# A gated delta rule in chunks on one Trainium2 core: three stages over couples instead of two, with rows of v and k made by TensorE

## The chip, the cores and the metric

The kernel runs on one core of one Trainium2 chip. The time is the device time of one whole execution in microseconds (us). The kernel before takes 4307.55 us, the median of 3 runs (4305.54 to 4310.32). TensorE is PE in the profile, its weight loads are PEld; VectorE is DVE, ScalarE is ACT, GpSimd is POOL, and SP issues the transfers.

## The reference, cut to what matters

Two layers run over 4096 tokens of width 256. The change touches one part, the gated delta rule of the first layer: 16 heads, keys and values of 64, one state of 64 x 64 for each head.

```
def step(S, inp):
    q_t, k_t, v_t, g_t, b_t = inp
    Sk = einsum('bhkv,bhk->bhv', S, k_t)
    delta = einsum('bhv,bhk->bhkv', v_t, k_t) - einsum('bhv,bhk->bhkv', Sk, k_t)
    S = exp(g_t)[..., None, None] * S + b_t[..., None, None] * delta
    o_t = einsum('bhkv,bhk->bhv', S, q_t)
    return (S, o_t)
_, o = scan(step, S0, (q, k, v, g, beta))      # then o @ Wo.T
```

The rest (norm and router, projections with a short convolution, experts, second norm, the last attention) is the same in both kernels.

## The kernel before, in words

The program is a row of phases, one after the other; `phase_delta` is the third. It works on chunks of C = 64 tokens, two chunks (x = 0 and 1) are a couple, and there are 32 couples. A tile `[P, NPAIR, C]` holds all 16 heads: two heads share the 128 partitions (64 each), 8 pairs lie along the free dimension. One "group" of TensorE work is `over_heads` over one `product`: 16 products of 64 x 64 by 64 x 64 in f32, all recorded at line 863, and the trace shows each product as two weight loads and two matmuls, so a group is 32 + 32 instructions. `over_heads` can take two products and then interleaves them one by one, which makes a pair of groups.

What is computed for a chunk: (1) `keys_keys`, the products of keys with keys, masked and scaled into `upper` (`take_upper`, `minus_eye`); (2) the inverse of that triangular matrix by five doublings, level k = 1 to 5, each `half` (PE), `mask_step` (DVE), `up` (PE), `turn_low` (DVE) and `keep_inverse` (ACT); (3) `keys_queries`, masked into `qk` (`attention`, DVE); (4) the state's part, a chain from chunk to chunk: `residual` (k_g times the state) into the bank `pd_r`, subtracted on DVE from the rows of v (L1180), `updates` (PE), `take_updates` (u, DVE L1193), `decay_updates` (u_dec = u times the decay, POOL L1301), `new_state` (k_row times u_dec, PE) and `take_state` (DVE L1198), beside it `old_outputs` and `new_outputs` into `pd_o`, and `project` (L939, 64 instructions of which half are matmuls of 256 columns) once a couple in two parts.

The rows of k and v come from elsewhere: k and v are loaded with the channel on the partitions, a transpose on DVE turns them in blocks of 32 (L1170, L1175), and ACT copies the blocks to their places in 8 small copies for each chunk and each of the two (L1100 `keep_rows`, L1109 `keep_values`).

The order is written out by hand and unrolled over 33 iterations. Iteration `it` has `post` = couple it (state part), `pre` = couple it+1 (inverse) and `ahead` = couple it+2 (its loads, decays, `grow`, `rel`). On PE `keys_keys(ahead)` is paired with the last `up` of `pre`, and masking and the first inverse follow at the top of the next iteration, in front of the first `half`. Every engine runs its own list in order and waits on semaphores; there is no loop instruction in the phase. SP issues all loads of a couple: 8 transfers of 128 KB (sums, sums_k), k, v and q of 512 KB each, and 128 KB of rows. The core of the list on PE at the top of an iteration:

```
new, asked = over_heads(updates(post, 0), keys_queries(pre, 1))
wait_half(pre, 0, 1);  wait_outputs(post, 0)            # the second waits for u
low, out = over_heads(half(pre, 0), new_outputs(post, 0))
wait_half(pre, 1, 1);  wait_new(post, 0)                # the second waits for u_dec
low, new = over_heads(half(pre, 1), new_state(post, 0))
```

Of the kernel before, what the change touches and what calls it, by code (L numbers as in the profile page):

```python
# [14 lines left out]
P = 128  # L15
T = 4096
D = 256
# [32 lines left out]
def shape_constants():  # L50
# [14 lines left out]
    for n in range(LEVELS):  # L65
# [6 lines left out]
        "couples": -couples - eye_c, "doublings": np.concatenate(doublings[1:], 1), "eye_c": eye_c,  # L72
        "iota": np.tile(np.arange(NE), (P, 1)).astype(float),
# [608 lines left out]
def phase_delta(nc, g, ctx):  # L682
# [19 lines left out]
    KEY_LOADS = 9  # L702
# [8 lines left out]
    upper = [sb(f"upper{x}", W) for x in range(2)]  # L711
    k_g = sb("k_g", [P, 4, NPAIR, C])
    qk = sb("qk", [P, 4, NPAIR, C])
    inv = [sb(f"inv{x}", W) for x in range(2)]
    inv_low = [sb(f"inv_low{x}", W) for x in range(2)]
    k_turned = [sb(f"k_turned{x}", W) for x in range(2)]
    v_turned = [sb(f"v_turned{x}", W) for x in range(2)]
    v_row = sb("v_row", [P, 2, NPAIR, C])
    step = [sb(f"step{x}", W) for x in range(2)]
    inv_fin = sb("inv_fin", [P, 4, NPAIR, C])  # L720
# [3 lines left out]
    u_dec = sb("u_dec", W)  # L724
# [10 lines left out]
    k_in, q_in, v_in = ([sem(f"{n}_in{r}") for r in range(2)] for n in "kqv")  # L735
# [4 lines left out]
    kt_d, vt_d, values_d, minus_d = (sem2(s) for s in ("kt", "vt", "values", "minus"))  # L740
    res_d, ress_d, w_d, u_d, udec_d, o_d, ocp_d = (sem(s) for s in ("res", "ress", "w", "u", "udec", "o", "ocp"))
# [3 lines left out]
    kk_d, qk_d, upper_d, att_d, inv1_d, rows_d = (sem2(s) for s in ("kk", "qk", "upper", "att", "inv1", "rows"))  # L745
# [3 lines left out]
    def heads():  # L749
        for p in range(NPAIR):  # L750
            for h in range(2):
                yield p, slice(h * C, (h + 1) * C)
# [7 lines left out]
    B32 = C // 2  # L760
    SAME, OTHER = range(2)

    def blocks_of(h):

        to = (1 - h) * C
        for a in range(2):
            for b in range(2):
                yield (slice(h * C + b * B32, h * C + (b + 1) * B32), slice(a * B32, (a + 1) * B32),
                       slice(to + a * B32, to + (a + 1) * B32), slice(b * B32, (b + 1) * B32))

    class Couple:


        def __init__(self, eng, c, odd, uses):
            keep = (lambda value: value) if isinstance(c, int) else eng.to_reg
            self.c, self.first = c, isinstance(c, int) and c < 2
            self.now, self.last = keep(c + 1), keep(c)
            self.level = [keep(c * NL + n) for n in range(NL + 1)]
            self.chunk = [c * 2 + x for x in range(2)]
            self.begun = [keep(c * 2 + x) for x in range(2)]  # L780
            self.ended = [keep(c * 2 + x + 1) for x in range(2)]
            self.stated = [keep(c * 2 + x + 2) for x in range(2)]
            self.older = None if self.first else [keep(c * 2 + x - 3) for x in range(2)]
            self.before = None if self.first else keep(c - 1)
            self.previous = [keep(c * 2 + x - 1) for x in range(2)] if c > 0 else None
            self.key_loads = keep(uses * (16 * KEY_LOADS))
            self.odd, self.filled = odd, keep(uses * 16)
            self.emptied = None if self.first else keep(uses * 32 - 32)
            self.ring = [odd * 2 + x for x in range(2)]

    def fixed(eng, c):
        return Couple(eng, c, c % 2, c // 2 + 1) if 0 <= c <= LAST else None

    def couples(engine, one):


        for it in range(-1, LAST + 1):
            one(fixed(engine, it), fixed(engine, it + 1), fixed(engine, it + 2))
# [3 lines left out]
    @block.sync  # L802
    def _(sp):
        sp.dma_start(wo[:], g.given["wo_t"].rearrange("(n p) d -> p n d", p=P)).then_inc(wo_in, 16)
# [5 lines left out]
        def load_keys(n):  # L810
            for x in range(2):
                for h in range(2):
                    for dst, half in ((sums, h), (sums_k, 1 - h)):
                        sp.dma_start(dst[half * C:(half + 1) * C, x].rearrange("p n t -> p (n t)"),
                                     spread(g.sums_d[bass.ds(n.chunk[x], 1), h, :], [C, NPAIR * C])).then_inc(k_in[n.odd], 16)
            load("k", k_t, n).then_inc(k_in[n.odd], 16)

        def load_rows(n):
            if not n.first:
                sp.wait_ge(scattered[n.odd], n.emptied)  # L820
            sp.dma_start(rows[:, n.odd, :], g.xn_d[bass.ds(n.c * P, P), :]).then_inc(rows_in[n.odd], 16)

        load_keys(fixed(sp, 0))
        load("q", q_t, fixed(sp, 0)).then_inc(q_in[0], 16)
        load("v", v_t, fixed(sp, 0)).then_inc(v_in[0], 16)
        load_rows(fixed(sp, 0))

        def one(post, pre, ahead):
            if ahead is None:
                return  # L830
            if post is not None:
                for x in range(2):
                    sp.wait_ge(qk_d[x], post.now)
                    sp.wait_ge(kt_d[x], post.now)
                    sp.wait_ge(kg_d[x], post.now)
                    sp.wait_ge(grow_d[x], post.now)
            if pre is not None:
                for x in range(2):
                    sp.wait_ge(diff_d[x], pre.now)
                    sp.wait_ge(grow_d[x], pre.now)  # L840
            load_keys(ahead)
            if post is not None:
                for x in range(2):
                    sp.wait_ge(vt_d[x], post.now)
            load("v", v_t, ahead).then_inc(v_in[ahead.odd], 16)
            if post is not None:
                sp.wait_ge(o_d, post.ended[1])
            load("q", q_t, ahead).then_inc(q_in[ahead.odd], 16)
            load_rows(ahead)

        couples(sp, one)
        for r in range(2):
            sp.wait_ge(scattered[r], (LAST + 1) // 2 * 32)

    @block.tensor
    def _(pe):
# [16 lines left out]

        def wait_keys(n, x):
            wait_each(pe, (k_in[n.odd], n.key_loads))

        def keys_keys(n, x, p, h):
            r = n.ring[x]
            return product(p, h, p_pre[x], OTHER, of_couple(k_t, r), of_couple(k_t, r))

        def wait_queries(n, x):
            wait_each(pe, (q_in[n.odd], n.filled), (up_d[x], n.level[0]))

        def keys_queries(n, x, p, h):
            r = n.ring[x]
            return product(p, h, p_low[x], OTHER, of_couple(k_t, r), of_couple(q_t, r))

        def wait_half(n, x, k):
            if k == 1:
                wait_each(pe, (minus_d[x], n.now))  # L890
            wait_each(pe, (lowc_d[x], n.level[k]))

        def half(n, x, p, h):
            return product(p, h, p_pre[x], SAME, of(upper[x]), of(inv_low[x]))

        def wait_up(n, x, k):
            if k == 1:
                wait_each(pe, (inv1_d[x], n.now), (att_d[x], n.now))
            else:
                wait_each(pe, (up_d[x], n.level[k - 1]))  # L900
            wait_each(pe, (step_d[x], n.level[k]))

        def up(n, x, p, h):
            return product(p, h, p_low[x], SAME, of(step[x]), of(inv[x]))

        def wait_state(n, x):
            wait_each(pe, (kg_d[x], n.now), (qg_d[x], n.now), (ocp_d, n.begun[x]), (state_d, n.ended[x]))

        def residual(n, x, p, h):
            return product(p, h, p_r, OTHER, of(k_g, n.ring[x]), of(state))  # L910

        def old_outputs(n, x, p, h):
            return product(p, h, p_o, SAME, of(state), of_couple(q_t, n.ring[x]), start=p == 0, stop=False, shared=True)

        def wait_updates(n, x):
            wait_each(pe, (tok_d, n.last), (up_d[x], n.level[NL]), (ress_d, n.ended[x]))

        def updates(n, x, p, h):
            return product(p, h, p_u, SAME, of(inv_fin, n.ring[x]), of(resid))

        def wait_outputs(n, x):
            wait_each(pe, (att_d[x], n.now), (u_d, n.ended[x]))

        def new_outputs(n, x, p, h):
            return product(p, h, p_o, OTHER, of(u), of(qk, n.ring[x]), start=False, stop=p == NPAIR - 1, shared=True)

        def wait_new(n, x):
            wait_each(pe, (rows_d[x], n.now), (udec_d, n.ended[x]))

        def new_state(n, x, p, h):  # L930
            return product(p, h, p_n, OTHER, of(k_row, x), of(u_dec))

        def project(n, pairs):
            out = p_u[:].rearrange("p n t -> p (n t)")
            if pairs[0] == 0:
                wait_each(pe, (wo_in, 16), (ocp_d, n.ended[1]))
# [7 lines left out]

# [1627 lines left out]
```

## Time and profile before

| what | value |
| --- | --- |
| median of 3 runs | 4307.55 us |
| the profiled execution's own time | 4308.53 us |
| its span (first to last instruction) | 4306.8 us |
| PE busy / PEld busy | 3878.8 us (90%) / 2318.4 us (54%) |
| DVE / ACT / POOL busy | 3062.9 / 2444.4 / 1101.5 us |
| instruction queue q8 | 424 packets, 6.95 MB |
| the delta phase | about 560 to 1800 us of the span |

The page gives busy time by engine, then the span in 40 slices (each digit a tenth), then the transfer queues. A busy PE is not a PE at its peak, since matmuls overlap. Queue q8 carries instructions, not data. The word "issue" in a row says that an engine stood idle while no semaphore that the profile knows held it.

### The profile page before, as it was taken

Reading aid. Unit: us, or ns where it says so; the run is one execution under the profiler, and the core shown is the slowest. Engines: PE = TensorE matmul, PEld = TensorE weight load, DVE = VectorE, ACT = ScalarE, POOL = GpSimd, SP = SyncE. Lnnn points to the kernel's source line nnn. Section 1 sums busy time; section 2 is a strip of 40 time slices with the busy share of each in tenths; the row PEclk is TensorE's granted clock in tenths of the full one; section 3 lists DMA queues with packets and bytes.
Section 4 is the critical chain, followed back from the end, with each engine's and each line's share of the span. In section 5 each row is a group of like instructions: output and inputs, shape, how many; then the busy total and the mean of one; then the engine's idle time right before and its main releaser. Section 6 shows DMA issues by size and latency. Waiting matters only on the chain. (4 is left out here: it accounts for less than half of the span.)

```text
span 4306.8 us, 128467 instructions
## 1 busy us (share of the span) xinstructions
PE 3878.8 (90%) x52237; PEld 2318.4 (54%) x52237; DVE 3062.9 (71%) x5127; ACT 2444.4 (57%) x3901; POOL 1101.5 (26%) x1106
## 2 busy tenths in 40 slices
PE   5999778888888788897887999999999999999998
PEld 4444377777777777676664344444444444444443
DVE  5799855555555555444896787878878787878786
ACT  2788655656655565434442465656656565656554
POOL 1000055655555555201777000000000000000000
PEclk9999889989899998999897899999999999999999
DMA  3544532222222222225345000000000000000000
GB/s 126 184 125 120 150 101 86 88 74 83 83 85 85 72 87 81 61 85 154 100 111 132 8 5 19 4 9 15 10 14 10 13 5 19 5 17 6 10 15 10
DMA packets 271802, 265.28 MB, mean 62 GB/s; under 512 B 53761, under 2 KB 232065, under 8 KB 270497
## 3 DMA queue, kind: packets, MB, share of 16 engines
q1 hardware_dynamic: 250768, 226.07, 17.6%
q0 software_dynamic: 6144, 16.79, 1.2%
q10 hardware_dynamic: 14352, 14.55, 1.0%
q8 instruction: 424, 6.95, 0.7%
q14 instruction: 114, 0.93, 0.1%
HBM read 151.95 MB, written 105.38 MB: 60 GB/s over the span
## 5 line engine op out<-in xcount | busy, mean ns | idle before, releaser
L2358 DVE TENSOR_REDUCE part_max<-p_m 128x1 f32<-128x512 f32 x2118 | 1362.9, 685 | 378.5 <-PE p_m L2200 371.0
L2340 ACT ACTIVATE prob<-p_s 128x1024 f32<-128x1024 f32 x1024 | 1047.7, 1023 | 748.2 <-PE p_s L2264 746.1
L2219 PE MATMUL p_o<-prob,v_one 128*64 128x512 f32 x4096 | 1054.6, 592 | 3.9 <-ACT prob L2340 0.5
L2200 PE MATMUL p_m<-keys,queries 96*64 96x512 f16 x4236 | 661.7, 387 | 28.0 <-DMA keys<-parts_d 20.4
L2264 PE MATMUL p_s<-queries,keys 97*64 97x512 f16 x4096 | 619.4, 380 | 0.0
L2264 PEld LDWEIGHTS p_s<-queries,keys 97*64 97x64 f16 x4096 | 228.8, 109 | 597.6 <-issue 592.8
L863 PE MATMUL pd_pre<-inv_low,upper 64*64 64x64 f32 x10240 | 397.3, 234 | 103.1 <-issue 56.5
L2168 POOL TENSOR_TENSOR attn<-o_num,o_inv 32x512 f32<-32x512 f32 x64 | 81.0, 1265 | 1458.6 <-DVE o_inv L2377 1452.1
L863 PEld LDWEIGHTS pd_pre<-inv_low,upper 64*64 64x64 f32 x10240 | 364.3, 147 | 120.7 <-issue 115.5
L2200 PEld LDWEIGHTS p_m<-keys,queries 96*64 96x64 f16 x4236 | 239.1, 108 | 309.9 <-DVE part_max L2358 56.3
L863 PE MATMUL pd_low<-inv,step 64*64 64x64 f32 x10240 | 373.2, 229 | 26.8 <-issue 24.9
L863 PEld LDWEIGHTS pd_low<-inv,step 64*64 64x64 f32 x10240 | 349.0, 144 | 59.6 <-issue 57.7
L2219 PEld LDWEIGHTS p_o<-prob,v_one 128*64 128x64 f32 x4096 | 288.4, 136 | 162.5 <-issue 15.8
L588 PE MATMUL p_proj<-xn_t_all,proj_w_sb 128*128 128x512 f32 x768 | 337.8, 596 | 7.7 <-PEq L2503 7.7
L1118 ACT ACTIVATE inv<-pd_low 128x512 f32<-128x512 f32 x256 | 152.7, 597 | 333.4 <-DVE inv_low L1212 332.4
L1204 DVE TENSOR_TENSOR step<-pd_pre,const 128x512 f32<-128x512 f32 x320 | 215.5, 679 | 85.9 <-PE pd_pre L863 82.0
L1212 DVE STREAM_TRANSPOSE inv_low<-pd_low 128x512 f32<-128x512 f32 x256 | 181.4, 709 | 127.9 <-PE pd_low L863 127.8
L588 PEld LDWEIGHTS p_proj<-xn_t_all,proj_w_sb 128*128 128x128 f32 x768 | 146.9, 191 | 192.9 <-issue 187.7
L1100 ACT ACTIVATE k_row<-k_turned 32x256 f32<-32x256 f32 x512 | 211.9, 414 | 6.9
L1109 ACT ACTIVATE v_row<-v_turned 32x256 f32<-32x256 f32 x512 | 211.8, 414 | 6.9
L1301 POOL TENSOR_TENSOR u_dec<-u,rel 128x512 f32<-128x512 f32 x64 | 67.7, 1058 | 290.8 <-DVE u L1193 290.8
L2377 DVE RECIPROCAL o_inv<-o_raw 128x64 f32<-128x64 f32 x256 | 137.8, 541 | 0.0
(235 smaller groups left out, 5725.2 us busy)
## 6 DMA issues: line engine op xcount, KB each, us to landing
q_d<-conv_q SPq DMA_DIRECT2D x16, 1024.0 KB, 5.0
v_d<-conv_v SPq DMA_DIRECT2D x16, 1024.0 KB, 5.0
k_d<-conv_k SPq DMA_DIRECT2D x16, 1024.0 KB, 6.5
sums<-sums_d SPq DMA_DIRECT2D x128, 128.0 KB, 3.1
sums_k<-sums_d SPq DMA_DIRECT2D x128, 128.0 KB, 3.4
k_t<-k_d SPq DMA_DIRECT2D x32, 512.0 KB, 4.9
q_t<-q_d SPq DMA_DIRECT2D x32, 512.0 KB, 3.6
v_t<-v_d SPq DMA_DIRECT2D x32, 512.0 KB, 5.3
```

Source lines behind the costliest of these rows:

```text
L588: last = te.matmul(p_proj[u % RING][:], g.proj_w_sb[:, n, c, p * P:(p + 1) * P], g.xn_t[:, c, b * BLK:(b + 1) * BLK], start=c == 0, stop=c ...
L863: return te.matmul(out[rows_of(h if to == SAME else 1 - h), p, :], lhs(p, rows_of(h)), rhs(p, rows_of(h)), start=start, stop=stop, skip_gr ...
L1100: last = a.activation(k_row[to_p, x, :, to_t], k_turned[x][from_p, :, from_t], ACT.Copy)
L1109: last = a.activation(v_row[to_p, x, :, to_t], v_turned[x][from_p, :, from_t], ACT.Copy)
L1118: a.activation(inv[x][:] if k < NL else inv_fin[:, n.ring[x]], p_low[x][:], ACT.Copy).then_inc(up_d[x], 1)
L1204: v.tensor_tensor(step[x][:], p_pre[x][:], over_pairs(masks[:, k - 1, :]), ALU.mult).then_inc(step_d[x], 1)
L1212: v.transpose(inv_low[x][:], p_low[x][:]).then_inc(lowc_d[x], 1)
L2200: last = te.matmul(p_m[k % 2][x * HALF:(x + 1) * HALF, :], queries[0:ROW, p, hh, at:at + HALF], keys[0:ROW, 2 * p + hh, kb * BLK:(kb + 1) ...
L2219: product = te.matmul(p_o[64 * hh:64 * hh + VW, :], g.v_one[:, j, p, hh:hh + 2, :].rearrange("p a d -> p (a d)"), prob[:, j % 2, hh, :], s ...
L2264: last = te.matmul(p_s[j % 2][x * HALF:(x + 1) * HALF, hh, :], keys[0:KR, 2 * p + hh, at:at + HALF], queries[0:KR, p, hh, :], start=True, ...
L2340: a.activation(prob[:, j % 2], p_s[j % 2][:], ACT.Exp, scale=SCORE_SCALE).then_inc(exp_d, 1)
L2358: v.tensor_reduce(part_max[:, hh * SUB + sub, kb:kb + 1], p_m[k % 2][:], AX.X, ALU.max).then_inc(red_d, 1)
```

## The change

`phase_delta` is written anew around the same arithmetic. The loop runs over 34 iterations from -2.

1. Stages: `keys_keys(ahead)` moves to the middle of the iteration, into the banks `pd_r` and `pd_n`, and `take_upper`, `minus_eye`, `first_inverse` and `turn_first` of `ahead` are done within the same iteration, two couples ahead of the state part; `upper` becomes a ring of four. The last-but-one inverse goes to a new tile `inv_half`.
2. Rows by TensorE: `key_rows` and `values` are products of k and v with the identity (`eye_c`, and a new constant `less_eye`, the negative). The 4 DVE transposes and 32 small ACT copies of a couple go; `take_rows` (DVE) multiplies the rows of k by the decay while it takes them from the bank, so that `decay_updates` on POOL goes and `new_state` waits for u alone.
3. `values` leaves minus v in `pd_r`, `residual` adds to it there, and ACT takes it with scale -1 (`residual` on ACT); the DVE subtraction goes.
4. The order on PE: nearly every group of the state part is paired with one of the inverse, 14 pairs and 10 groups alone. The order before has 9 pairs and 16 groups alone.
5. Loads: sums, k, sums_k, v, rows, q, each behind its own wait. The bytes are the same.

```
+    def values(n, x):
+        return lambda p, h: product(p, h, p_r, OTHER, of_couple(v_t, n.ring[x]), of_const("less_eye"), start=p == 0, stop=False, shared=True)
+    def key_rows(n, x):
+        return lambda p, h: product(p, h, p_o if x == 0 else p_n, OTHER, of_couple(k_t, n.ring[x]), of_const("eye_c"))
+    def residual(n, x):                                   # PE
+        return lambda p, h: product(p, h, p_r, OTHER, of(k_g, x), of(state), start=False, stop=p == NPAIR - 1, shared=True)
-    v.tensor_tensor(resid[:], v_row[:, x], p_r[:], ALU.subtract).then_inc(ress_d, 1)
+    a.activation(resid[:], p_r[:], ACT.Copy, scale=-1.0).then_inc(ress_d, 1)
+    v.tensor_tensor(k_row[:, x], (p_o if x == 0 else p_n)[:], spread(rel[:, n.ring[x], :, C:C + 1], W), ALU.mult)
-    po.tensor_tensor(u_dec[:], u[:], spread(rel[:, n.ring[x], :, C:C + 1], W), ALU.mult).then_inc(udec_d, 1)
```

The new list on PE, a line for each group or pair (the semaphore waits ahead of each are left out):

```
half(pre,0)+residual(post,0)      half(pre,1)+keys_queries(pre,0)
old_outputs(post,0)               updates(post,0)+values(post,1)
up(pre,0,1)                       up(pre,1,1)+new_outputs(post,0)
half(pre,0)+new_state(post,0)     half(pre,1)
up(pre,0,2)+residual(post,1)      up(pre,1,2)+keys_queries(pre,1)
old_outputs(post,1)               updates(post,1)
half(pre,0)                       half(pre,1)+new_outputs(post,1)
up(pre,0,3)+new_state(post,1)     up(pre,1,3)+keys_keys(ahead,0)
half(pre,0)+keys_keys(ahead,1)    half(pre,1)+key_rows(pre,0)
project, first part               up(pre,0,4)+key_rows(pre,1)
up(pre,1,4)+values(pre,0)         half(pre,0)   half(pre,1)
project, second part              up(pre,0,5)   up(pre,1,5)
```

## Rows read from the trace of the kernel before

**Rows 1.** The page: busy time, then the slices of PE and its granted clock.
```profile
PE 3878.8 (90%) x52237; PEld 2318.4 (54%) x52237; DVE 3062.9 (71%) x5127; ACT 2444.4 (57%) x3901; POOL 1101.5 (26%) x1106
PE   5999778888888788897887999999999999999998
PEclk9999889989899998999897899999999999999999
```

**Rows 2.** Stretches: length, busy us (instructions) of each engine, clock, transfer share, GB/s.
```profile
560.00:1780.00 1220.00, 1014.29 (x35249) 923.99 (x35248) 704.58 (x1075) 716.80 (x1534) 694.02 (x653) 0.92 0.25 78
1365.60:1380.90 15.30, 13.89 (x509) 13.34 (x508) 10.83 (x17) 9.02 (x20) 6.24 (x7) 0.89 0.18 53
1433.90:1439.87 5.97, 2.87 (x126) 2.63 (x127) 1.99 (x3) 5.18 (x13) 1.63 (x2) 1.00 0.61 196
1419.30:1424.90 5.60, 5.44 (x125) 4.67 (x126) 2.23 (x4) 2.37 (x5) 4.59 (x5) 1.00 0.12 31
1467.14:1469.20 2.06, 2.06 (x71) 1.99 (x66) 1.88 (x3) 1.19 (x2) 0.81 (x1) 1.00 0.03 8
1471.03:1473.10 2.07, 2.07 (x141) 2.07 (x143) 0.69 (x1) 0.98 (x2) 0.46 (x2) 1.00 0.65 216
```

**Rows 3.** One line's instructions, once a couple: duration ns, first and last start.
```profile
L1134 ACT ACTIVATE attn_tok<-pd_u x32: 383/383/387, 619.7 to 1805.6; 128x256 f32<-128x256 f32 x32
```

**Rows 4.** Transfer queues, stretch 560 to 1780: packets, MB, share of 16 engines.
```profile
q1 hardware_dynamic: 36514, 82.65, 21.2%
q8 instruction: 279, 4.57, 1.6%
```

**Rows 5.** Order of time, PE: start, us, group, count, idle before it and releaser.
```profile
1421.87 1.95 PE L939 MATMUL pd_u<-wo,o_t 128*64 128x256 f32 x16
...
1439.87 0.21 PE L863 MATMUL pd_u<-resid,inv_fin 64*64 64x64 f32 x1 [3.07 <-issue]
...
1459.25 0.62 PE L863 MATMUL pd_pre<-inv_low,upper 64*64 64x64 f32 x13
1461.64 1.73 PE L863 MATMUL pd_pre<-inv_low,upper 64*64 64x64 f32 x51 [1.78 <-issue]
...
1489.19 0.32 PE L863 MATMUL pd_pre<-inv_low,upper 64*64 64x64 f32 x4
1490.91 0.51 PE L863 MATMUL pd_pre<-inv_low,upper 64*64 64x64 f32 x10 [1.40 <-issue]
```

**Rows 6.** Transfer queues, stretch 1365.6 to 1380.9.
```profile
q8 instruction: 4, 0.07, 2.2%
```

**Rows 7.** Transfer queues, stretch 1432.5 to 1437.5, whole answer's queue part.
```profile
DMA packets 499, 1.38 MB, mean 277 GB/s; under 512 B 72, under 2 KB 72, under 8 KB 499
q1 hardware_dynamic: 499, 1.38, 88.2%
```

**Rows 8.** Waits, 560 to 1780: us in total, times, longest.
```profile
PE pd_pre L863 <- issue: 59.1, 55, 2.6
PE pd_low L863 <- issue: 49.8, 63, 3.8
PE pd_pre L863 <- DVE u L1193: 29.4, 30, 1.2
PE pd_o L863 <- issue: 20.1, 17, 2.7
```

**Rows 9.** Groups of instructions, 560 to 1780: busy us, mean ns, idle before.
```profile
L1109 ACT ACTIVATE v_row<-v_turned 32x256 f32<-32x256 f32 x504 | 208.5, 414 | 6.8
L1180 DVE TENSOR_TENSOR resid<-v_row,pd_r 128x512 f32<-128x512 f32 x62 | 42.6, 687 | 54.1 <-PE pd_r L863 54.1
L1123 ACT ACTIVATE o_t<-pd_o 128x512 f32<-128x512 f32 x62 | 36.9, 595 | 52.4 <-PE pd_o L863 52.2
L1301 POOL TENSOR_TENSOR u_dec<-u,rel 128x512 f32<-128x512 f32 x62 | 65.6, 1058 | 270.4 <-DVE u L1193 270.4
L1297 POOL TENSOR_TENSOR inv<-upper,const 128x512 f32<-128x512 f32 x62 | 78.6, 1267 | 4.4
```

More of the change, by code:

```diff
@@ L791, in fixed, with __init__ @@
[L791 to L798, printed above, removed]
+    class Couple:
+        def __init__(self, c):
+            self.c, self.odd = c, c % 2
+            self.now, self.last, self.before = c + 1, c, c - 1
+            self.level = [c * NL + n for n in range(NL + 1)]
+            self.chunk = [c * 2 + x for x in range(2)]
+            self.begun = [c * 2 + x for x in range(2)]
+            self.ended = [c * 2 + x + 1 for x in range(2)]
+            self.previous = [c * 2 + x - 1 for x in range(2)]
+            self.older = [c * 2 + x - 3 for x in range(2)]
+            self.filled = (c // 2 + 1) * 16
+            self.emptied = c // 2 * 32
+            self.ring = [self.odd * 2 + x for x in range(2)]
@@ L800, in phase_delta, with couple, couples @@
+    def couple(c):
+        return Couple(c) if 0 <= c <= LAST else None
+    def couples(one):
+        for it in range(-2, LAST + 1):
+            one(couple(it), couple(it + 1), couple(it + 2))
     block = ctx.enter_context(nc.Block())
@@ L808, in load @@
             return sp.dma_start(dst[:, n.odd].rearrange("p n x t -> p n (x t)"), src)
[L810 to L826, printed above, removed]
         def one(post, pre, ahead):
@@ L903, in up @@
[L903 to L913, printed above, removed]
@@ L960, in first_part, with one @@
-        def first_part(post, pre):
+                    for i, one_product in enumerate(products):
+                        if one_product is not None:
+                            last[i] = one_product(p, h)
+            return last
+        def one(post, pre, ahead):
+            if pre is not None:
+                wait_half(pre, 0, 1)
             if post is not None:
-                wait_state(post, 0)
-                _, last = over_heads(lambda p, h: old_outputs(post, 0, p, h), lambda p, h: residual(post, 0, p, h))
-                last.then_inc(res_d, 1)
+                wait_residual(post, 0)
+            low, res = over_heads(half(pre, 0) if pre is not None else None, residual(post, 0) if post is not None else None)
@@ new lines, in one @@
+            if post is not None:
+                wait_old(post, 0)
+                over_heads(old_outputs(post, 0))
+                wait_updates(post, 0)
+                wait_values(post, 1, None)
+                new, kept = over_heads(updates(post, 0), values(post, 1))
+                new.then_inc(w_d, 1)
+                kept.then_inc(val_d, 1)
+            if pre is not None:
+                wait_up(pre, 0, 1)
+                over_heads(up(pre, 0, 1))[0].then_inc(upmm_d[0], 1)
+                wait_up(pre, 1, 1)
@@ L1069, in _ @@
-        for x in range(2):
-            wait_keys(fixed(pe, 0), x)
-            over_heads(lambda p, h: keys_keys(fixed(pe, 0), x, p, h))[0].then_inc(kk_d[x], 1)
+                wait_old(post, 1)
+                over_heads(old_outputs(post, 1))
+                wait_updates(post, 1)
+                over_heads(updates(post, 1))[0].then_inc(w_d, 1)
+            if pre is not None:
+                wait_half(pre, 0, 3)
+                over_heads(half(pre, 0))[0].then_inc(half_d[0], 1)
+                wait_half(pre, 1, 3)
@@ new lines, in one @@
+            if post is not None:
+                wait_outputs(post, 1)
+            low, out = over_heads(half(pre, 1) if pre is not None else None, new_outputs(post, 1) if post is not None else None)
+            if pre is not None:
+                low.then_inc(half_d[1], 1)
+            if post is not None:
+                out.then_inc(o_d, 1)
+            if pre is not None:
+                wait_up(pre, 0, 3)
+            if post is not None:
+                wait_new(post, 1, pre)
+            raised, new = over_heads(up(pre, 0, 3) if pre is not None else None, new_state(post, 1) if post is not None else None)
@@ new lines, in one @@
+            if pre is not None:
+                raised.then_inc(upmm_d[0], 1)
+            if post is not None:
+                new.then_inc(new_d, 1)
+            if pre is not None:
+                wait_up(pre, 1, 3)
+            if ahead is not None:
+                wait_keys(ahead, 0)
+            raised, keyed = over_heads(up(pre, 1, 3) if pre is not None else None, keys_keys(ahead, 0) if ahead is not None else None)
+            if pre is not None:
+                raised.then_inc(upmm_d[1], 1)
@@ new lines, in one @@
+            if pre is not None:
+                wait_half(pre, 1, 4)
+                wait_key_rows(pre, 0, ahead)
+                low, turned = over_heads(half(pre, 1), key_rows(pre, 0))
+                low.then_inc(half_d[1], 1)
+                turned.then_inc(kr_d[0], 1)
+            if post is not None:
+                project(post, range(0, NPAIR // 2))
+            if pre is not None:
+                wait_up(pre, 0, 4)
+                wait_key_rows(pre, 1, ahead)
+                raised, turned = over_heads(up(pre, 0, 4), key_rows(pre, 1))
+                raised.then_inc(upmm_d[0], 1)
+                turned.then_inc(kr_d[1], 1)
+                wait_up(pre, 1, 4)
+                wait_values(pre, 0, ahead)
+                raised, kept = over_heads(up(pre, 1, 4), values(pre, 0))
+                raised.then_inc(upmm_d[1], 1)
+                kept.then_inc(val_d, 1)
+                for x in range(2):
+                    wait_half(pre, x, 5)
+                    over_heads(half(pre, x))[0].then_inc(half_d[x], 1)
@@ L1072, in _ @@
+            if post is not None:
+                project(post, range(NPAIR // 2, NPAIR))
+            if pre is not None:
+                for x in range(2):
+                    wait_up(pre, x, 5)
+                    over_heads(up(pre, x, 5))[0].then_inc(upmm_d[x], 1)
         pe.wait_ge(g.const_in, 16)
-        couples(pe, one)
+        couples(one)
     @block.scalar
@@ L1126, in one @@
             if post is not None:
-                keep_rows(post, 0)
-                keep_values(post, 1)
-                keep_outputs(post, 0)
-                keep_rows(post, 1)
-            for k in range(1, NL + 1):
-                if k == NL and post is not None:
-                    act.wait_ge(proj_d, post.now)
-                    a.activation(g.attn_tok[:, bass.ds(post.c, 1), :].rearrange("p a d -> p (a d)"),
-                                 p_u[:].rearrange("p n t -> p (n t)")[:, 0:D], ACT.Copy).then_inc(tok_d, 1)
-                if pre is not None:
+                residual(post, 0)
@@ new lines, in one @@
+            if pre is not None:
+                for x in range(2):
+                    grown(pre, x)
+            if ahead is not None:
+                related(ahead, 0)
+            if pre is not None:
+                for x in range(2):
+                    keep_inverse(pre, x, 1)
+            if post is not None:
+                keep_outputs(post, 0)
+            if ahead is not None:
+                related(ahead, 1)
+            if post is not None:
+                residual(post, 1)
@@ L1137, in one @@
+            if pre is not None:
+                for x in range(2):
+                    keep_inverse(pre, x, 2)
+            if post is not None:
+                keep_outputs(post, 1)
+            if pre is not None:
+                for k in (3, 4):
                     for x in range(2):
                         keep_inverse(pre, x, k)
[L1139 to L1143 removed]
@@ L1144, in one @@
-                if k == 3:
-                    if post is not None:
-                        keep_outputs(post, 1)
-                    if ahead is not None:
-                        for x in range(2):
-                            related(ahead, x)
-        for x in range(2):
-            grown(fixed(act, 0), x)
-            related(fixed(act, 0), x)
-        couples(act, one)
+            if post is not None:
+                act.wait_ge(proj_d, post.now)
+                a.activation(g.attn_tok[:, bass.ds(post.c, 1), :].rearrange("p a d -> p (a d)"),
+                             p_u[:].rearrange("p n t -> p (n t)")[:, 0:D], ACT.Copy).then_inc(tok_d, 1)
@@ L1156, in _ @@
+            if pre is not None:
+                for x in range(2):
+                    keep_last_inverse(pre, x)
+        couples(one)
     @block.vector
```

556 lines of the change are left out of this document (267 added, 289 removed).

## The prediction

> **What bounds the kernel now.** I read the page first, for where the time is: PE is busy nearly everywhere, and from about slice 6 to slice 17, where the clock digit drops to 8 and 9, runs the only phase that the change touches [rows 1]. The stretch view gives its size: 1220 us between 560 and 1780, PE busy 1014 of them, DVE 705, ACT 717, POOL 694 [rows 2]. Three engines are idle for 40% of it, so PE's list sets the time, and the question is what holds PE.
>
> The period first. `attn_tok` is written once a couple, 32 times between 619.7 and 1805.6 [rows 3]; that is 38.3 us a couple, and as the last iteration is a short one (the state part alone), about 38.7 for a full iteration. In it PE executes 34 groups of 64 instructions and 64 of `project`, 2240. What would they take if nothing but the array counted? Two groups alone, one behind the other, took 2.06 us, and two pairs 2.07 us for twice the instructions, the last two rows of their group [rows 2]. So a group alone and a pair both cost 1.03 us: the second member of a pair is free for the array. `project` took 1.95 us a part [rows 5]. Before: 16 alone + 9 pairs = 25 x 1.03 + 2 x 1.95 = 29.7 us. The 9.0 us to 38.7 are what has to be explained.
>
> The waits name little of it: 29.4 us in all are for u, 0.95 us a couple; most of the rest is "issue", 59.1 + 49.8 + 20.1 us and smaller ones [rows 8]. The order of time shows what those are. At 1459.9 PE stops after 13 matmuls of a row of `half` and goes on with the next at 1461.64; no semaphore stands inside a group. At 1489.5 the same for 1.40 us, and in the middle of an `updates` for 3.07 us [rows 5]. The transfer queues give the cause: q8, which carries instructions, moved 279 packets in the 1220 us, 4.57 MB, so 16 KB each [rows 4]. PE executed 35249 + 35248 instructions there [rows 2], 253 to a packet, with the semaphore waits beside them about 256 of 64 bytes. One block of instructions lands every 4.37 us on average. Four blocks were fetched and 1017 instructions executed in a calm stretch of 15.3 us, 3.83 us each, and in that stretch both paired and single groups ran [rows 2, 6]. One block took 5.97 us with PE busy for 2.87 of them; for 5 us of that, k, v and sums kept the transfer engines 88% busy and q8 moved nothing [rows 7]. One took 5.60 us because it held a part of `project`, whose few instructions are long [rows 2].
>
> So I read it thus: **PE is fed at about 3.83 us for a block of 256 instructions**, whether these are paired (the array would need 1.8 us) or not (3.7 us), and more when a burst of loads or long instructions fall in. By that, before is 2240 / 253 = 8.86 blocks x 3.83 = 33.9 us, and 4.8 us of excess: bursts, `project`, the waits for u and u_dec.
>
> The Trainium skill says otherwise of the price: the page Runtime: NRT & Kernel Launch, section Instruction fetch mechanics, has blocks of 16 KiB, 256 instructions, fetched ahead while the current one runs, at a cost "mostly hidden". The trace agrees with the size of the block and not with the hiding: 1.40 and 1.78 us of standstill in the middle of a group [rows 5]. What the rule would make of this change is the fourth rival.
>
> **The change part by part.**
>
> *Groups on PE.* `values` and `key_rows` add 2 + 2 groups a couple: 256 instructions, all in pairs. For the array they are free: 14 pairs + 10 alone = 24 x 1.03 + 3.9 = 28.6 us, 1.1 less than before. For the feeding they are a full block: 2496 / 253 = 9.87 blocks. Price of a block between 1.84 us (pairs at the array's rate, 2.07 x 253 / 284) and 5.97 (in a burst); I take the calm stretch's 3.83, since it has the mix of both kinds: 9.87 x 3.83 = 37.8, **+3.9 us a couple**.
>
> *What goes from PE's path.* `new_state` waits no more for u_dec (POOL, 1.06 us, behind other POOL work [rows 9]), and between `updates` and `new_outputs` a group `up` is put (1.03 us), which covers the 0.69 us of u: the 0.95 us a couple of waits for u go, **-0.95**. The u_dec wait lies mostly inside the fetch of the same block, as the top of the iteration is also where the loads burst [rows 7]; I count 0 for it, and -1.1 at the most.
>
> *`project`.* Its first part now has pairs on both sides, 1.95 us + 221 instructions at pair rate (1.6) = 3.6, below 3.83, so its block costs no more than any other; the second still has `half` and `up` alone round it. The block with a part cost 5.60 against 3.83 but the next one then comes early, so of the 1.8 I take half: **-0.9**. Ends: 0 and -1.8.
>
> *The other engines.* ACT loses 32 small copies of 414 ns a couple, 13.2 us, and gets 2 of about 0.6 for the residual; DVE loses 4 transposes and 2 subtractions of about 0.68 and gets 2 `take_rows`; POOL loses 2 x 1.06 [rows 9]. All three idle 40% now, PE waits for them rarely, so 0. The covers stay: ACT's residual is 0.60 instead of DVE's 0.69 and has `old_outputs` (1.03) beside it.
>
> *Moved steps and added waits.* `pd_n` now serves in turn `keys_queries`, `new_state`, `keys_queries`, `new_state`, `keys_keys`, `key_rows`, each waiting for DVE to empty it: 6 x (1.15 + 0.69) = 11 us of turns in a period near 40. The tightest is `keys_keys(ahead, 1)`, which waits for `take_state(1)` one pair after `new_state(1)`; `half` of level 4 is queued behind it. By the array's rate it would stand up to about 1 us; fed at 3.83 a block (a pair each 1.9) the wait is over when its instructions come. I take 0, upper end +1. POOL's list is about 21 us an iteration (18 operations of 1.05 to 1.28, [rows 9], and the scatter), DVE's 24 x 0.69: neither is near 40. `first_inverse` (1.27 us on POOL, [rows 9]) and `turn_first` leave the top, where the first `half` follows them; as that is where the burst holds the block anyway, 0, with -1.3 as the end.
>
> *Loads.* Same 2.9 MB a couple, asked for in another order: sums, k and sums_k still together at the top. The bursts, 2 to 2.5 blocks a couple, stay: 0, from -1 (spread out) to +1 (k, v and sums meet more fetches). Start and end: one more short iteration, but the same chain to the first `half`: 0, +/- 5 us once. 64 more constant columns: 32 KB, nothing.
>
> *Sum.* 3.9 - 0.95 - 0.9 = +2.05 us a couple, 40.8 in place of 38.7; x 31 full iterations = +64 us. On the profiled execution's 4308.5 us (span 4306.8) that is 4372; this execution is 1.0 us above the median of the runs, which changes nothing I can claim. **Forecast 4372 us.**
>
> **The rivals.**
> 1. *The excess grows with the blocks.* Each block costs the average 4.37 us, not 3.83 plus a fixed rest: 9.87 x 4.37 = 43.1, +4.4 x 31 = +137: **4445**. For: a burst hits whichever fetch is under way, and with shorter work a block more of them end in a standstill. Against: the waits for u are plainly not tied to blocks.
> 2. *Faster: the chain's waits were the excess.* The mechanism is the top of the iteration, `updates`, u, u_dec, `new_state` in single file: if they, and not the loads, made the 5.97 us blocks, the whole 4.8 goes as the new order covers them all: 37.8, -0.9 x 31 = **4280**. It decides from the point where more than 3.9 of the 4.8 us go. For: u_dec waited 270 us for u, PE for both. Against: q8 moved nothing for 5 us while data did [rows 7], and the long block ran to its end on the fetch.
> 3. *A draw.* 3.9 gained and lost: **4308**.
> 4. *Blocks are hidden*, and PE's standstills have another cause which thinner lists of ACT and DVE remove: 28.6 us of array work and some 2 of waits, -8 x 31: **4060**. Against: standstills inside a group.
>
> **How the numbers follow.** Forecast 0.50; rival 1 0.17; rival 2 0.22; draw 0.07; rival 4 0.04. This kernel's measurement can tell 0.2%, 8.6 us, from no change. Slower: 0.50 + 0.17, faster: 0.22 + 0.04 and 0.01 of the draw, same 0.06. The range takes the forecast's open terms (-1.1 - 0.9 - 1 to +0.9 + 1 + 1 a couple, not all at once) and reaches into both neighbours: 4275 to 4455.
>
> **What would show it.** PE's instructions in the phase up by 8192, q8's packets in it by about 32, to some 310. The period of `attn_tok` from 38.3 to 40 or 41. "Issue" idle of PE up by 30 us or more with standstills inside pairs, the row of PE waiting for u gone, ACT's and DVE's busy time down by 380 and 80 us without effect. Wrong would be: blocks coming faster than 3.5 us on average, or a period under 38.

## The result, and the profile after

The changed kernel takes 4340.39 us (median of 4 runs, 4335.22 to 4350.06), the kernel before beside it 4308.93 us: ratio 1.0076, 95% interval 1.0055 to 1.0097. It is 31 us slower, where 64 were forecast. On the chip of a later batch the kernel before took 4358 us and the changed one 4346 us, a ratio of 0.9979 (0.9968 to 0.9991): there the change is a small gain. The changed kernel is nearly the same on both (4340, 4346); it is the kernel before that moved by 49 us. So each experiment below is read against the kernel before of its own batch, and as a difference: the times in the expectations reckon from 4309 or 4340 us. The granted clock goes with it: over a whole run it is 0.952 to 0.957 in the kernel before where it takes 4305 and 0.944 to 0.949 where it takes 4358, and 0.964 to 0.971 in the changed kernel on either.

The page after, the same three lines as [rows 1]:

```profile
PE 3834.0 (88%) x56333; PEld 2258.0 (52%) x56333; DVE 2981.2 (69%) x4999; ACT 2057.0 (47%) x2941; POOL 1035.6 (24%) x1042
PE   5999777777777777799687999999999999999998
PEclk9999899999999999999898899999999999999999
```

PE has 4096 more matmuls and 4096 more weight loads, and is busy 45 us less; ACT is busy 387 us less, DVE 82 us less, and none of that came back as time. The stretch of the phase, columns as in [rows 2]:

```profile
560.00:1820.00 1260.00, 965.71 (x38977) 859.25 (x38978) 617.43 (x940) 333.09 (x590) 627.28 (x589) 0.96 0.24 76
```

The line written once a couple, against 619.7 to 1805.6 in [rows 3]:

```profile
L1204 ACT ACTIVATE attn_tok<-pd_u x32: 384/384/386, 619.5 to 1845.9; 128x256 f32<-128x256 f32 x32
```

That is (1845.9 - 619.5) / 31 = 39.56 us a couple, 1.31 more than 38.25. The start is the same to 0.2 us, and from the last of these lines to the end of the span it is 2502.4 us against 2501.2: the whole difference of the two profiled executions (4350.06 and 4308.53 us) lies in the iterations of the delta phase.

The waits of PE, same view as [rows 8], over 560 to 1800:

```profile
PE pd_pre L836 <- issue: 79.4, 56, 3.4
PE pd_low L836 <- issue: 69.1, 57, 2.1
PE pd_n L836 <- issue: 45.8, 40, 2.4
PE pd_o L836 <- issue: 25.7, 23, 2.6
PE pd_r L836 <- issue: 25.2, 24, 2.1
PE pd_low L836 <- DVE step L1255: 10.9, 17, 1.2
PE pd_pre L836 <- DVE state L1249: 8.5, 13, 1.4
```

The row of 29.4 us for u is gone, and what DVE still holds PE for is 19 us in the last two. "Issue" has grown: the five rows of it shown here alone are 245 us, where all of it in the phase was 161 before. Order of time, PE, in the middle of a pair of `half` and `key_rows`:

```profile
1413.85 0.22 PE L836 MATMUL pd_pre<-inv_low,upper 64*64 64x64 f32 x1
1413.86 0.22 PE L836 MATMUL pd_o<-const,k_t 64*64 64x64 f32 x1
1417.09 0.27 PE L836 MATMUL pd_pre<-inv_low,upper 64*64 64x64 f32 x1 [3.01 <-issue]
1417.10 0.27 PE L836 MATMUL pd_o<-const,k_t 64*64 64x64 f32 x1
```

PE stands 3.2 us from the start of one instruction to the start of the next of the same pair, in the new work itself. Counting PE's instructions in the trace, waits included, and cutting them in blocks of 256, 247 of the 309 blocks that begin between 560 and 1820 have over 0.1 us between the 256th instruction of the block before and their own first; in the kernel before it was 146 of 279 (560 to 1780). Shifting the cut by any other number of instructions makes the idle time at the cuts almost vanish, 6 us and less. Added up over the phase, PE is idle 274 us at these block ends and 44 us elsewhere; before it was 130 and 113 us. So the feed held the old kernel for about half of its idle time only, and holds the new one for most of it (also in its later run on the other chip, with 221 and 78 us). The queue that fetches instructions, over 560 to 1820 (packets, MB, share of the transfer engines' time):

```profile
q8 instruction: 309, 5.06, 1.7%
```

And the stretch right after that standstill, the end of the pair and the 16 matmuls of one part of `project`: its granted clock is 0.55, near the level of 1.2 GHz. The 16 matmuls take 3.4 us of it, for the work that took 1.95 before:

```profile
1417.24:1421.00 3.76, 3.76 (x32) 1.87 (x28) 1.29 (x2) 0.00 (x0) 0.00 (x0) 0.55 0.02 4
```

Over the whole execution q8 fetched 457 blocks in place of 424, 33 more for 32 couples.

### The profile page after: what moved, and what is told of

Its sections match the earlier page's. It is cut to its first block and busy times, and to the rows that moved or that the text cites. A ratio compares the mean times of both kernels' runs of the same rounds, so it can differ in the third digit from the quotient of the medians.

```text
span 4348.3 us, 135609 instructions
## 1 busy us (share of the span) xinstructions
PE 3834.0 (88%) x56333; PEld 2258.0 (52%) x56333; DVE 2981.2 (69%) x4999; ACT 2057.0 (47%) x2941; POOL 1035.6 (24%) x1042
## 5 line engine op out<-in xcount | busy, mean ns | idle before, releaser
L836 PE MATMUL pd_pre<-inv_low,upper 64*64 64x64 f32 x10240 | 386.6, 226 | 97.3 <-issue 80.4
L836 PEld LDWEIGHTS pd_pre<-inv_low,upper 64*64 64x64 f32 x10240 | 351.6, 140 | 104.3 <-issue 92.8
L836 PE MATMUL pd_low<-inv,step 64*64 64x64 f32 x8192 | 313.6, 226 | 83.5 <-issue 70.1
L836 PEld LDWEIGHTS pd_low<-inv,step 64*64 64x64 f32 x8192 | 284.5, 140 | 83.8 <-issue 82.0
L1163 ACT ACTIVATE inv<-pd_low 128x512 f32<-128x512 f32 x192 | 114.6, 597 | 336.4 <-DVE inv_low L1264 333.0
L1163 ACT ACTIVATE inv_half<-pd_low 128x512 f32<-128x512 f32 x64 | 38.3, 598 | 262.9 <-DVE inv_low L1264 262.9
L972 PE MATMUL pd_u<-wo,o_t 128*64 128x256 f32 x1024 | 138.7, 415 | 4.2 <-issue 4.2
L658 DVE SCALAR_TENSOR_TENSOR conv_k<-raw,conv_w_sb,conv_k 128x2048 f32<-128x2048 f32 x48 | 112.2, 2351 | 22.9 <-ACT raw L632 21.8
```

The source lines that it names most:

```text
L836: return te.matmul(out[rows_of(h if to == SAME else 1 - h), p, :], lhs(p, rows_of(h)), rhs(p, rows_of(h)), start=start, stop=stop, skip_gr ...
L972: last = te.matmul(out[x * C:(x + 1) * C, 0:D], o_t[:, x, p, :], wo[:, p, :], start=p == 0, stop=p == NPAIR - 1)
L1163: a.activation(inv_half[x][:] if k == NL - 1 else inv[x][:], p_low[x][:], ACT.Copy).then_inc(up_d[x], 1)
```

## The experiments

The first four ran on a chip where the kernel before took 4362.13 us.

**More blocks in the kernel before.**

```
+ pe.wait_ge(state_d, post.stated[1])
- halves(pre, 4)  ...  halves(pre, 5)
+ over_heads(half(pre, x), product(p, h, p_n, OTHER, eye, eye))   # levels 4 and 5, both x
```

> The kernel before with four groups more a couple (256 PE instructions), each paired with a half of level 4 or 5 that was alone; they multiply a constant with itself into pd_n while that bank is free, nobody reads them, and one wait (the state taken) stands ahead of the first. Theory F (PE is fed its instructions, one block of 256 at a time, about 4 us each): one block more a couple, +3.8 to +4.4 us x 31, so 4425 us (4400 to 4450). Theory A (the array and the chain of semaphores set the period; the second member of a pair costs the array nothing): +0 to +10 us, 4310 to 4320 us.

Measured 4447.13 us, ratio 1.0184 (1.016 to 1.0207), +85 us; q8 fetched 455 blocks, 31 more. Theory A is out: work that the array does beside other work, and whose result nobody reads, cost 2% of the kernel. F is right in sign and too high in size: 85 / 31 = 2.7 us for one more block, not 3.8 to 4.4. Part of even this may be the clock, which I did not separate: its mean is 0.938 in these runs and 0.946 in the kernel before beside them. The stretch from 700 to 1700 of the kernel before (on the other kind of chip), then of this run, columns as in [rows 2]:

```profile
700.00:1700.00 1000.00, 829.39 (x28873) 753.63 (x28874) 575.23 (x879) 591.98 (x1269) 576.40 (x543) 0.92 0.26 82
700.00:1700.00 1000.00, 802.70 (x28707) 721.34 (x28705) 517.02 (x782) 525.83 (x1127) 513.72 (x483) 0.87 0.23 73
```

The clock is 0.87 in the second row and 0.92 in the first.

**Fewer instructions in the changed kernel.**

```
- over_heads(half(pre, 1), key_rows(pre, 0))
+ over_heads(half(pre, 1), thin(key_rows(pre, 0), pre))   # thin: only p == 0; likewise key_rows(1), values(0), values(1)
```

> The changed kernel with key_rows and values cut to the first of eight pairs from the third couple on: 56 of the 64 instructions of each of the four groups are left out (so rows of k and v are stale for the other heads); all waits, readers and banks stay. F: 224 instructions less a couple, 0.88 block x 4.08 us x 30 couples = -107 us, 4233 us (4220 to 4260). A: the groups left out were second members of pairs, 0 for the array: 4340 us (4330 to 4345).

Measured 4284.7 us, ratio 0.9817 (0.9792 to 0.9842); the changed kernel unedited has 4346.12 us and 0.9979 in the next batch, where the kernel before takes nearly the same (4358), so -61 us (-70 by the ratios) for 27 blocks less (430): 2.3 to 2.6 us a block. Again only F moves at all, and again by about two thirds of what it said. The mean granted clock is the same here as in the changed kernel unedited (0.965 and 0.968), so no change of the clock is in this price. Between 700 and 1700 q8 fetches 235 blocks here and 246 there: with fewer blocks to fetch, each one left takes longer, 4.26 us against 4.07.

**Stages and order alone, rows as before.**

```
- raised, turned = over_heads(up(pre, 0, 4), key_rows(pre, 1))          # PE
+ v.transpose(k_turned[x][:], k_t[:, n.odd, :, x, :])                   # DVE, v likewise
+ a.activation(k_row[to_p, x, :, to_t], k_turned[x][from_p, :, from_t], ACT.Copy)   # 8 a chunk, v likewise
+ po.tensor_tensor(k_row[:, x], k_row[:, x], spread(rel[..., C:C + 1], W), ALU.mult)  # POOL, off the chain
- a.activation(resid[:], p_r[:], ACT.Copy, scale=-1.0)
+ v.tensor_tensor(resid[:], v_row[:, x], p_r[:], ALU.subtract)
```

> The changed kernel with its stages and order, but the rows of k and v made as before (DVE transposes, 32 ACT copies a couple), the residual subtracted on DVE, and the decay put on the rows of k by POOL off the chain. The whole result is computed. F: 2240 instructions, 8.86 blocks x 4.08 = 36.2 us a couple against 38.25 of before: 4308 - 2.1 x 32 = 4241 us (4220 to 4280). A: the array has the same work as in the changed kernel and ACT and DVE have more: 4340 us or above, up to 4400 if ACT's 13 us of copies stand in front of the inverse.

Measured 4248.6 us, ratio 0.9738 (0.972 to 0.9757). It was run again on a chip where the kernel before takes 4305 us:

> The stages and order of the changed kernel with rows by copies, unedited, beside the next two and to see its ratio once more: 0.970 to 0.978 times the kernel before where that takes 4358 us, 0.982 to 0.988 where it takes 4309.

Measured 4238.53 against 4304.93 us, ratio 0.9845 (0.9829 to 0.9862). This version beats both kernels on either chip. Its line once a couple:

```profile
L1208 ACT ACTIVATE attn_tok<-pd_u x32: 383/383/384, 615.2 to 1743.4; 128x256 f32<-128x256 f32 x32
```

36.39 us a couple, where F said 36.2. It has the blocks of the kernel before (424) and the order of the changed one. Its ACT is as loaded as before (731 us in a phase of 1180), and no row of the waits of PE names it. So the change comes apart in two: the stages and the order are worth 66 us where the kernel before takes 4305 (4305 - 4239) and 109 to 114 where it takes 4358 or 4362, and the rows by TensorE take 98 to 102 back on either (4346 - 4249, 4340 - 4239). With 33 blocks more, that is 3.0 to 3.1 us a block, a third price.

**Without u_dec in the kernel before.**

```
- product(p, h, p_n, OTHER, of(k_row, x), of(u_dec))
+ product(p, h, p_n, OTHER, of(k_row, x), of(u))        # decay of the updates left out; no decay_updates on POOL
```

> The kernel before with u_dec left out (new_state multiplies u itself, the decay of the updates is missing from the state): the POOL step of 1.06 us and its queue go from the chain u, u_dec, new_state, state. F with the excess of the top blocks made by bursts of loads: 0 to -1.1 us a couple, 4300 us (4275 to 4310). Rival (the 5.97 us blocks at the top were the chain's waits): -2.1 us a couple and more, 4240 us or lower.

Measured 4344.07 us, ratio 0.9951 (0.9933 to 0.997): -18 us, 0.6 us a couple. Inside F's range; the chain's rival of 66 us is out. The trace of this run is from a chip where the kernel before takes 4362 us: `attn_tok` starts at 618.3 and ends at 1839.4, 35 us more than in [rows 3] although there is less to do, so what such a chip adds lies in the delta phase.

The next four ran where the kernel before took 4357.78 us.

**The changed kernel again.**

> The changed kernel unedited, on the chip that runs the three below, since the kernel before took 4362 us where the first four ran and 4309 us where the changed kernel was first timed. If the ratio holds: 1.005 to 1.010 times the kernel before. If what is slow on the other chip is the feeding of instructions, the changed kernel suffers by more blocks and less chain: still 1.00 to 1.02.

Measured 4346.12 us, ratio 0.9979 (0.9968 to 0.9991), outside both expectations: below 1. What is slow there costs the changed kernel 6 us at the most.

**Loads cut, in both kernels.**

```
- dma_start(dst[:, n.odd] ..., src)                       # k, q, v
+ dma_start(dst[0:8, n.odd] ..., src[0:8])                # of couple n.odd, from the third couple on
- dma_start(dst[half * C:(half + 1) * C, x] ...)          # sums, sums_k
+ dma_start(dst[half * C:half * C + 4, x] ...)            # of chunk x, from the second couple on
```

> The changed kernel with the loads of the delta phase cut to 4 of 64 and 8 of 128 partitions from the second or third couple on (the state runs over the data of the first two couples; the stated waits and the count of transfers stay). F with bursts of loads delaying the fetch of a block: the 128 blocks that began with the transfer engines over 5% busy took 0.4 to 1.0 us more than the 115 calm ones, so -68 us (-45 to -90) on the changed kernel. Rival (bursts do not matter to PE): 0 to -10 us.

> The same cut in the kernel before. F: 75 blocks that began in a burst took 0.8 us more than the calm ones: -60 us (-35 to -90) on the kernel before. Rival (the long blocks at the top of the iteration were the waits for u and u_dec): 0 to -10 us, the blocks there stay above 5 us.

Measured 4296.62 us (0.9854, 0.9838 to 0.9871) for the changed kernel, -49.5 us; and 4296.45 us (0.9857, 0.9841 to 0.9873) for the kernel before, -61 us. Bursts of loads do cost time in both, as F said; once they are gone the two kernels are level. The waits of PE in the kernel before without its loads, columns as in [rows 8], show what lay under the bursts:

```profile
PE pd_pre L867 <- issue: 38.2, 57, 1.8
PE pd_pre L867 <- DVE inv_low L1212: 35.3, 19, 2.1
PE pd_o L867 <- issue: 31.3, 68, 1.5
PE pd_pre L867 <- DVE u L1197: 30.1, 30, 1.2
```

"Issue" is 104 us in all rows, against 161 with the bursts (and on the other kind of chip), and semaphores hold it more: 65 us in the rows of DVE, where the inverse was 9.8 us and u 29.4. The phase is hardly shorter by it, 1180.5 us from the first line of `attn_tok` to the last against 1185.9: what the feed gives back beside the kernel before of the first chip is mostly taken up by semaphores and by a busier PE, as feed waits and chain waits lay over each other. What the cut saves on such a chip was not run; the 61 us hold for a chip where the kernel before takes 4358.

**Loads in one bunch in the changed kernel.**

```
+ if ahead.c > 1: sp.wait_ge(val_d, ahead.ended[1] - 4)   # moved from ahead of v to ahead of all loads
```

> The changed kernel with the wait for the bank of v moved ahead of all loads of a couple, so that sums, k, sums_k and v are asked for in one bunch in the first third of the iteration, as in the kernel before, instead of spread from the middle of the one before. F: the spread loads are part of why the change cost 31 us and not 64: +15 to +45 us on the changed kernel. Rival: the spread does nothing, 0 (-5 to +5).

Measured 4387.69 us, ratio 1.0072 (1.0055 to 1.009): +41.6 us on the changed kernel, inside what F said. One wait moved on SP, no instruction of a computing engine touched. Its line and its q8 (700 to 1700):

```profile
L1204 ACT ACTIVATE attn_tok<-pd_u x32: 383/384/385, 621.3 to 1878.4; 128x256 f32<-128x256 f32 x32
```
```profile
q8 instruction: 239, 3.92, 1.7%
```

That is (1878.4 - 621.3) / 31 = 40.55 us a couple. But the number agrees with F for another reason. The waits of PE, ACT and POOL, 700 to 1700, have rows that the unedited changed kernel lacks:

```profile
PE pd_low L836 <- ACT inv L1163: 72.3, 24, 6.5
ACT rel L1152 <- POOL rel L1330: 257.1, 48, 13.1
POOL rel L1328 <- DMA sums<-sums_d: 359.3, 24, 17.0
```

The moved wait also holds back `sums`. POOL waits for it, ACT's `rel` waits for POOL, and as `rel` stands ahead of `keep_inverse` in ACT's list, PE waits for the inverse, 3.0 us once a couple. The rows of "issue" are 135 us in this stretch, against 197 in the unedited kernel. So a chain of semaphores that starts at late `sums` is more than enough for the 41.6 us, and this run does not show what bunched loads cost the instruction feed.

The last four ran beside a kernel before of 4304.93 us.

**The kernel before again.**

> The kernel before unedited, for its trace on a chip where it takes about 4358 us and not 4309. If the difference is the feeding of PE's instructions behind bursts of loads: same standstills at the blocks' ends, same waits on u, the blocks that begin in a burst longer than 4.77 us, or more of them; the other phases the same within 5 us. If it is something else: other phases longer too.

Measured 4303.8 us, ratio 0.9997 (0.9986 to 1.0008). This chip is of the kind of the first, so the trace repeats the first (blocks that began with the transfer engines over 5% busy took 4.73 us, the others 4.13; 4.76 and 4.15 in the first) and says nothing of the chips where it takes 4358.

**Pairs taken apart.**

```
- for p ...: for h ...: for i, one_product in enumerate(products): last[i] = one_product(p, h)
+ for i, one_product in enumerate(products): for p ...: for h ...: last[i] = one_product(p, h)
```

> The kernel of the stages with rows by copies, but over_heads gives out its products one group behind the other instead of interleaved, same instructions and waits. A (array): 34 groups alone x 1.03 + 3.9 = 38.9 us a couple where 24 slots x 1.03 + 3.9 = 28.6 were, so the ten second members now cost 10.3 us x 32 if the array had set the time: +330 us. F (feeding): the period was 36.4 already, above what pairs need, so only what the array now needs beyond it: 38.9 + 0 to 1.5 against 36.4, +80 to +130 us on that kernel.

Measured 4247.38 us, ratio 0.9863 (0.9847 to 0.988), +9 us on the version it is made from. The 9 us are near the spread of the runs. Both expectations are too high; A's 330 us by a factor of 37. Two stretches of 1000 us (700 to 1700), paired first, then one behind the other:

```profile
700.00:1700.00 1000.00, 814.22 (x30376) 732.51 (x30373) 592.43 (x921) 623.48 (x1324) 597.70 (x564) 0.97 0.27 84
```
```profile
700.00:1700.00 1000.00, 929.01 (x30328) 859.73 (x30327) 604.07 (x919) 624.50 (x1327) 597.36 (x563) 0.99 0.27 84
```

PE is busy 115 us more in the same time and executes the same number of instructions: 60749 and 60655. That is 237 blocks of 256 in 1000 us for both. The unpaired groups fill what were standstills. The waits of PE over the same 1000 us, paired first, then unpaired:

```profile
PE pd_pre L850 <- issue: 49.3, 39, 3.6
PE pd_n L850 <- issue: 41.6, 36, 3.7
...
PE pd_low L850 <- issue: 31.2, 34, 2.4
```
```profile
PE pd_n L850 <- issue: 24.5, 25, 2.9
...
PE pd_pre L850 <- issue: 13.5, 23, 1.4
```

My array price for groups alone was also off: the period here is 36.3 us, (1742.2 - 616.3) / 31, and holds 34 groups and `project`, so a group alone takes at most (36.3 - 3.9) / 34 = 0.95 us on average, not 1.03. The array and the feed need nearly the same here, so the run says that the pairing buys next to nothing, and no more.

**Loads cut in the version with rows by copies.**

> The kernel of the stages with rows by copies, with the loads of the delta phase cut to 4 of 64 and 8 of 128 partitions (the state runs over the data of the first two couples). F with bursts: as in the changed kernel, -50 us (-30 to -65). Rival (its blocks are no longer held by the feed but by ACT's copies and DVE): 0 to -15 us.

Measured 4193.96 us, ratio 0.9741 (0.9724 to 0.9757), -44.6 us: bursts delay its blocks too.

## Why the prediction was right or wrong

*What bounds the kernel: right for the changed kernel, half right for the one before.* Added instructions that cost the array next to nothing cost 85 us, removed ones gave 61, and the order without pairs cost 9. The idle time at the block ends (274 of 318 us, before 130 of 243) says how far the feed holds each. The page's "mostly hidden" (Runtime: NRT & Kernel Launch, Instruction fetch mechanics, of the Trainium skill) does not hold here: the size of a block agrees, the hiding does not.

*The count of blocks: right.* +33 of 457, against 32 said. The other signs came as said ("issue" up from 161 to 266 us, the row for u gone), but for the period: 39.6 us where I wanted 40 or 41.

*The price of one more block: the term that was mis-sized.* I took the whole cost of a calm block, 3.83 us, so +121 us. By the version with rows by copies this part is some 100 us, 3.0 to 3.1 us a block; the other two experiments gave 2.7 (31 more) and 2.3 to 2.6 (27 fewer). An average is not a marginal price. The counts fit this reading: from the kernel before to the changed one the idle time at block ends rose by 144 us and the rest fell by 69, so part of the new standstills took the place of old waits. Which old wait met which fetch was not followed.

*The staging: under-priced.* -0.95 - 0.9 = -1.85 us a couple is -57 us; measured are -66 where the kernel before takes 4305. So the 64 us forecast came out as 35 (-66 + 101; 31 beside its own kernel before) because the block cost 20 less and the staging gave 9 more. Where the kernel before takes 4358 the same staging gives 109 and the sign of the whole turns. The forecast knew nothing of such chips; that its sign came true is in part the luck of the chip.

*What the staging consists of.* u's 29.4 us left the waits of PE. u_dec, priced at 0 with -1.1 as the end, is 0.6 us by its own experiment in the kernel before. The -0.9 for `project` is not shown: the blocks that hold a part of it went from 4.90 to 4.71 us on average, but those that hold none from 4.24 to 3.91, so its surcharge did not shrink; after a long standstill it now runs at 1.2 GHz, as in the stretch above.

*The loads: 0 is not shown to be wrong.* They do cost both kernels time, 49.5 and 61 us by the cut loads, both where the kernel before takes 4358, but about the same. Their difference of 12 us is 0.4 us a couple, inside the ends of -1 to +1. Blocks in whose first 1 us the transfer engines were over half busy were 74 of 282 before and 55 of 313 after. The run that bunches them again does not count here, as it made PE wait for the inverse. One reading of mine was off: the 5 us of [rows 7] begin 1.4 us ahead of the long block, so 3.6 us of them lie in it. The next fetch then starts at 1437.60, right behind the burst, and PE goes on at 1439.86.

*The calm price.* The 3.83 us are from one stretch of four blocks. Over the phase of the kernel before, the blocks that began calm took 4.15 us on average, in the changed one 3.89.

*The other engines: right at 0.* 387 us less on ACT bought nothing that shows, and the version that gives them back to ACT is the fastest with the whole result.

*The rivals.* 4340 is as near to the draw (4308) as to the forecast (4372). Rival 1 (4445, each block at the average of 4.37 us) and rival 4 (4060, blocks hidden) are out by the prices above. Rival 2 (4280) wanted the whole excess to be waits of the chain; without u_dec the kernel before gains 18 us and not 66, but the order that covers such waits gave 66 to 114 us once the added block was left out, so there was more in it than I thought.

*Open:* why the kernel before needs 49 us more on some chips while the changed one needs 6. With loads cut both take 4296 on that chip, and the extra time comes with a lower granted clock in the kernel before alone (0.947 for 0.954); whether the transfers or the clock are the cause is not shown, as no unedited trace of the kernel before from such a chip was taken.

## What to carry to other kernels

Where a phase is unrolled and its work is thousands of small matmuls, count instructions a period before busy time: divide them by what one fetch of the instruction queue holds, compare with the fetches' spacing, and look for standstills inside a group. Moving work to TensorE "for free" in the second half of a pair is then not free, and idle ACT and DVE are the right place for it. Price an added block below the average (here 2.3 to 3.1 us of 4.1 to 4.4) and take the exact price from one run that adds dummies, with an eye on the granted clock. Split a change into its parts with one kernel that has only some of them: here that version is 2.3% faster than the change itself. Loads cost the instruction feed some time too (45 to 61 us here). And when a run gives the number that was expected, read its waits before taking the reason as well: bunching the loads cost what the theory said, by a chain of semaphores that the theory did not have.

## What the runs showed of the hardware

- Between 700 and 1700 us PE executes 57700 instructions in the kernel before, 61600 in the changed one and 64400 in that with loads cut, with 229, 244 and 255 fetches of 16 KB; with and without pairs it is 60700 in both. The time from the start of a fetch to the first instruction of its block was 2.5 us (median) when PE stood waiting for it.
- The next fetch started 1.1 us after a block began in calm and 2.5 us after it with the transfer engines over 80% busy in the first 1 us (medians, 33 such blocks of the kernel before).
- After 3.2 us without a new instruction PE ran a part of `project` at a granted clock of 0.55 and took 3.4 us for what took 1.95 at full clock.
- Chips differ: by 1.2% on the kernel before and by 0.1% on the changed one, between the ones that these runs met.
